# New orders of the steps on every engine of a four-layer network kernel on one core

## The reference

```python
x = _layernorm(x + _L0_attn_ref(x, ...))   # 16 heads of 64, softmax attention
x = _layernorm(x + _L0_ffn_ref(x, ...))    # hard routing: best of 8 clusters, best of its 8 tiles, spline of that tile
x = _layernorm(x + _L1_attn_ref(x, ...))   # linear attention and attention in a window of 65, gated; out @ wo + bo + x
x = _layernorm(x + _L1_ffn_ref(x, ...))    # causal attention with normalised q and k, then a mixture of 8 experts
```

## Time and profile before

| what | us |
|---|---|
| median of 3 runs | 2324.85 (2324.02 to 2327.23) |
| the profiled execution, its own time | 2327.11 |
| span of its trace | 2325.3 |
| mean granted clock of TensorE | 0.989 of full speed |
| PE busy | 2189.3 (94%) |
| DVE busy | 1605.0 (69%) |
| ACT busy | 1352.6 (58%) |
| POOL busy | 849.2 (37%) |

### The profile page before, as it was taken

One profiled execution on the slowest core, in us unless ns is written; L12 is line 12 of the kernel. 1 busy time (PEld: TensorE's weight loads), 2 busy tenths in 40 slices (PEclk: granted clock), 3 DMA queues, 4 the chain that ended last, 5 costly groups with the idle time before them and its releaser, 6 DMA issues.

```text
span 2325.3 us, 44711 instructions
## 1 busy us (share of the span) xinstructions
PE 2189.3 (94%) x16091; PEld 1523.0 (65%) x16091; DVE 1605.0 (69%) x5015; ACT 1352.6 (58%) x3784; POOL 849.2 (37%) x1010
## 2 busy tenths in 40 slices
PE   8989999999999999999999999999999999999897
PEld 5656666856668566676667665676666756667465
DVE  5666686686766866678765878658686686766752
ACT  5336574765647755476555767466564764646452
POOL 3314561054510654107521256114561054510630
PEclk9999999999999999999999999999999999999999
DMA  4000001010010100110001100001001010010001
GB/s 153 28 1 1 1 2 46 11 33 1 1 55 2 33 1 1 55 33 1 1 10 46 33 1 1 28 28 33 1 1 46 10 33 1 2 42 6 33 1 50
DMA packets 24726, 50.48 MB, mean 22 GB/s; under 512 B 3316, under 2 KB 3900, under 8 KB 24252
## 3 DMA queue, kind: packets, MB, share of 16 engines
q1 hardware_dynamic: 24508, 47.63, 6.3%
HBM read 45.52 MB, written 2.10 MB: 20 GB/s over the span
## 4 chain that ended last, share of the span: by engine, by line
PE 81%; DVE 9%; ACT 5%; POOL 3%; issue 1%; DMA 0%; SPq 0%; DVEq 0%; ACTq 0%
PE ps L1488 10%; PE ps L1509 10%; PE ps L601 5%; PE ps L667 5%; PE ps L650 4%; PE ps L1521 4%; PE ps L867 4%; PE ps L1422 4%; PE ps L1439 4%; PE ps L905 4%; PE ps L1394 3%; PE ps L798 3%; PE ps L781 3%; PE ps L834 3%; PE ps L1383 2%; PE ps L605 2%
## 5 line engine op out<-in xcount | busy, mean ns | idle before, releaser
L1047 POOL TENSOR_TENSOR rstd<-ve,half_neg 128x4 f32<-128x4 f32 (+1 forms) x56 | 66.8, 1193 | 972.4 <-DVE ve L1028 972.4
L1509 PEld LDWEIGHTS ps<-wbuf,QK 128*128 128x128 f32 x2048 | 265.4, 191 | 108.2 <-issue 103.3
L1304 POOL TENSOR_TENSOR E<-E,ri 128x512 f32<-128x512 f32 x240 | 249.4, 1041 | 149.7 <-DVE ri L1102 148.8
L1612 ACT ACTIVATE QK<-ps,cols 128x512 f32<-128x512 f32 x256 | 173.9, 687 | 219.3 <-PE ps L1488 218.9
L1738 POOL TENSOR_TENSOR work<-work,ri 128x128 f32<-128x128 f32 x480 | 231.6, 506 | 108.7 <-DVE ri L1661 107.0
L1488 PE MATMUL ps<-h2T,wbuf 128*128 128x512 f32 x512 | 270.9, 617 | 0.1
L1509 PE MATMUL ps<-wbuf,QK 128*128 128x128 f32 x2048 | 269.0, 275 | 0.0
L928 ACT ACTIVATE E<-ps,nm 128x256 f32<-128x256 f32 x480 | 224.5, 479 | 57.9 <-DVE nm L1095 56.9
L1731 POOL TENSOR_TENSOR rn<-ss,half_neg 128x8 f32<-128x8 f32 x120 | 196.0, 1638 | 156.5 <-DVE ss L1637 154.0
L1572 ACT ACTIVATE work<-ps,nm 128x128 f32<-128x128 f32 x480 | 200.2, 433 | 66.9 <-DVE nm L1653 66.0
L1653 DVE CUSTOM_DVE_ANT_0 ps<-ps,causal 128x128 f32<-128x128 f32 (+1 forms) x512 | 167.5, 389 | 31.0 <-PE ps L1422 30.1
(11 more groups left out here) (280 smaller groups left out, 4558.6 us busy)
## 6 DMA issues: line engine op xcount, KB each, us to landing
wbuf<-in_w SPq DMA_DIRECT2D x128, 256.0 KB, 3.2
xT<-in_xT SPq DMA_DIRECT2D x8, 256.0 KB, 3.5
xr<-in_xr SPq DMA_DIRECT2D x8, 256.0 KB, 3.8
bias_t<-in_bias_t SPq DMA_DIRECT2D x1, 2048.0 KB
out_y<-xn SPq DMA_DIRECT2D x8, 256.0 KB, 2.1
wqkv<-in_wqkv SPq DMA_DIRECT2D x1, 1536.0 KB
wo<-in_wo SPq DMA_DIRECT2D x2, 512.0 KB, 7.8
rows<-in_rows SPq DMA_DIRECT2D x1, 531.0 KB, 6.6
```

The source lines that it names most:

```text
L1304: nc.gpsimd.tensor_tensor(L.E[:, g % 4, :, :], L.E[:, g % 4, :, :], L.ri[:, g, :].unsqueeze(2).broadcast_to((P, NT, S)), ALU.mult)\
L1509: last = nc.tensor.matmul(bank2[2 + x % 2][:, t * P:(t + 1) * P], hid[:, x % 2, c, t * P:(t + 1) * P], w2[:, x % WB, c, :], start=(c == 0) ...
```

## The change

Only digits in `ORDER` differ: the tables of the joined parts for all five engines, and those of the last part for vector, tensor, scalar and gpsimd. The tables of part 0 are as they were. Every table keeps its length and its count of each digit, so every engine issues the same instructions in each part, and each half keeps its own order; only the interleaving is another. Entries that differ, of all: joined parts vector 132 of 458, tensor 104 of 337, scalar 90 of 294, gpsimd 36 of 95, sync 2 of 12; last part vector 58 of 229, tensor 64 of 176, scalar 52 of 157, gpsimd 14 of 53. Counted along a table, no step is moved by more than two steps of the other half.

```diff
--- before.py
+++ after.py
@@ -59,45 +59,45 @@
...
     ("both", "vector"):
-        "010001111011010101011110001111110110111111110110100111101110011111010100110110100010101101010011"
-        "110101110100001101101000011110011000100101010110110111111111011101111111111111011111111011110111"
-        "111011111011110011010000111100001001110100001101101000101100101010011100101000101101001001011010"
-        "001101000100101010100100000011111101111110001000000000000001000000000000100000110000000000000000"
-        "010100000110000100000110001010000100000000101011111110101100001001000010",
+        "001000101111101101101110001111110110111111101101100111101111011101001101001111000010111001100011"
+        "110011101100010110101000110101001010100011100110111011110111111101111111111111011111111101111110"
+        "111101110111101011010000101110001010110100010011101001011100010010010111010000101101001001010110"
+        "001010100110010101000110000001111101101010110100000000000000000000100000100000001000001000000000"
+        "100000010000100010010101101000000000010001011101011110101100000101000010",
     ("last", "vector"):
-        "000000010000001011101001011101010100110111101010101111111111101100001111101001011010100010010101"
-        "101001000111010001011011000101101100100110110010011011001001110100010111001001010100101010000000"
+        "000000000001001011101010111011010001101101011010111111110110111010111010110100101001010100001011"
+        "011000100111010001011011001001101100010111010010011011001001110100010111010001101000100110000000"
...
     ("both", "tensor"):
-        "010011111011011100101101011101110101110110101110010101010100111101010110101101010110010101110001"
-        "101011111011101011111011011101101110110110101110100101100010111101001010110101010011001010110101"
-        "001101001010110101010101010100111001100101111111111111101111111110111100110110110011000000000000"
-        "0000010000000100000000202000020000202200222222",
+        "001101101111011100101101101101101011110110110110010100110101101101011101001101010011011001011110"
+        "010101110111011011111101110101101110110110110101100010111101011100010100101011101010110010010101"
+        "001011010010110011011001011000101101100101111111111110111111111101111101001111010011000000000000"
+        "0000000010001000000000202000002000202202022222",
     ("last", "tensor"):
-        "000010010010010110110101000111010110110111111100110011011000100101001110100101010101100101101010"
-        "010110100101100101101010101000011100110000000000000000000000000000000000000000",
+        "000100001010001111011010101100101010111111110110001011000110110100101100001110100110100101100101"
+        "011010101010110001010011011000010111010000000000000000000000000000000000000000",
...
     ("both", "scalar"):
-        "110110001111010101011110111001111100100011111100011110000111101110100101110000101101101111111011"
-        "101011111111101111011110101100111010111010010110100110110001101010010110100011101001101001010110"
-        "011010100111011111111011111111111110111010111010101010000000000000000000000000000000022202022222"
+        "110010111110100101111100101011101110101101011010011010010101111110100011100101110100111101111110"
+        "101111011111110111110101101101101010111000101110001111001001011001010110010101100011011010011011"
+        "100100010110111111101111111111111101111010110110101010000000000000000000000000000000020220222222"
         "222",
     ("last", "scalar"):
-        "000000001001110101010011011011100111011101011001111000001011100101101010011100000111100101101100"
-        "00111001011010110010000000000000001000000000000000000000000",
+        "000000100011010101101100101101011011101011010011011010010110101001011010010110100101100101011001"
+        "00111010011011001001001000000000000000000000000000000000000",
...
     ("both", "gpsimd"):
-        "000110110111100001010111010110101010111111111111100110101001101010101001100101011010000010010",
+        "000111011011100001101001110101110001111111111111101010011011010001110001010101011001000001100",
     ("last", "gpsimd"):
-        "000101101101110011010100101010101100101101010100000",
+        "000101101101110011010010110100110101001011001100000",
     ("both", "sync"):
-        "1111101111",
+        "1101111111",
 }
 KINDS = ["first", "both", "both", "last"]
```

## The result

The changed kernel takes 2336.4 us in the median of its runs (2332.14 to 2346.52), the kernel before, beside it, 2327.37 us (2320.91 to 2336.36). The ratio is 1.0044, 95% interval 1.0027 to 1.0062: it is slower, by 6 to 14 us. The forecast was +7.2 us, to 2332, with a range of 2319 to 2342.

A forecast was written before the change was run, and what follows sets the result against it. The prediction took TensorE as the bound, busy 2189.3 of 2325.3 us. It summed 5.1 - 0.7 + 2.8 = +7.2 us onto the 2324.85 us median, giving 2332 us, with an 8-in-10 range of 2319 to 2342.

The forecast's parts named there:

- signs of being wrong: L899 starting with L650's end, L899 to L1422 over 0.5 us shorter, change mostly in last part, or other fall counts.
- (b): Opening of joined parts: power ahead of L1304 moves the POOL/DVE conflict; 0.1 us gained a part, 0.7 us in all.
- (a): End of joined parts 1 to 6: L601 between the L856 steps delays L899; 6 x 0.85 = 5.1 us lost.
- (c): Dense stretches of joined parts: new waits such as L867 on L1304; 0.4 us a part, 2.8 us lost.
- (d): Routing in the middle of joined parts: L718 two expert steps earlier, inputs just ready; cost 0, at most 0.5 a part.
- (e): Last part: opening bound by POOL's sixteen L1731, whose order stays; 0, with 1 us to either side.
- the clock falls at the boundary: Rival: wider PE wait at six boundaries halves the clock behind L899; up to 1.7 us each, +10, 2342 us; chance 0.15.

The follow-up runs named there:

- e1: Kernel before with only the new tail of the joined parts' tensor table (an L601 step between the two L856); ratio 1.0046, +7.2 us at equal clock.
- e2: Changed kernel with the old tail put back in the joined parts' tensor table; ratio 1.0018 to the kernel before, +0.4 us at equal clock.
- e3: Kernel before with two steps of the program ahead (four L601 pairs) between the two L856 steps; ratio 1.0087, +12.0 us at equal clock.
- e12: Changed kernel with idle PE matmuls in five idle places of each joined part; ratio 1.0006 to the kernel before, +7.1 us at equal clock.
- e7: Kernel before, old tables, with idle PE matmuls in five idle places of each joined part; ratio 0.9971, -1.2 us at equal clock.
- e5: Kernel before with the new tail alone, plus three idle matmuls ahead of the wait before L899; ratio 1.0060, +5.7 us at equal clock.
- e6: Kernel before with the double tail, plus six idle matmuls ahead of the wait before L899; ratio 1.0106, +11.2 us at equal clock.
- e9: Kernel before, old tables, with three idle matmuls (0.73 us) among the experts of each joined part; ratio 1.0053, +5.9 us at equal clock.
- e8: Kernel before, unchanged, profiled a second time; 2329.67 us.
- e10: Kernel before, old tables, with seven idle matmuls (1.7 us) among the experts of each joined part; ratio 1.0065, +11.0 us at equal clock.

## Why the prediction was right, and where it was not

The direction, the size and the place were right: +7.2 us forecast, +5.9 at equal clock, 1.0044 in all. That the +10 us of the ratio also lie near +7.2 is in part luck: the forecast had no clock in its sum. Two of its own signs of being wrong came: the first L1422 stands 0.54 us earlier in a part (under (b)), and the profile has more falls, ten in the joined parts against six. Neither touches the term that carries the sum.

(a) *The end of a joined part* is the cause, shown by one table entry alone (e1), by its removal (e2) and by twice the dose (e3). The forecast said 6 x 0.85 = 5.1 us; the wait grew by 5.0, and by 10.2 for the double. Part 7, without the program ahead, did not grow (281.0 us after 281.3), as said; one execution tells that to about 0.7 us only, since e1's part 7, with the old order inside and the same two falls, took 282.0. What made it readable in advance was the 0.06 us between DVE's last L1038 and L899 in the earlier trace rows. Nothing of the earlier L601 came back, as said.

(b) *The opening* was right in its mechanism, but its gain was put too small. L1394's wait for L1643 fell by 3.1 us, seven times 0.43, as worked out from the earlier trace rows. L867's wait for POOL's L1304 rose by 2.4 us, seven times 0.35. The forecast said only that it would not shrink. These two come to the 0.1 us a part of the forecast, but they are not the whole opening. The forecast put the end of the earlier trace rows at 786.0 after 786.07, as POOL is full; POOL's two L1304 came earlier too:

```profile
793.89 2.04 POOL L1304 TENSOR_TENSOR E<-E,ri 128x512 f32<-128x512 f32 x2
...
794.99 0.66 PE L867 MATMUL ps<-ident,E 128*128 128x128 f32 x4 [0.54 <-POOL E L1304]
```

This L867 stands 24.6 us into its part (from 770.4), where that of the earlier trace rows stood at 25.0 (from 761.1): 0.4 us gained, not 0.1. The first L1422 of a part came at 26.74 us after 27.28. DVE's L1637 of 0.81 us is gone, and a later one is held up behind an L1304 instead (timeline of after):

```profile
787.68 1.04 POOL L1304 TENSOR_TENSOR E<-E,ri 128x512 f32<-128x512 f32 x1
...
788.31 0.44 DVE L1637 TENSOR_SCALAR ss<-ss 128x8 f32<-128x8 f32 x1
```

That agrees with the rule of the Trainium skill, page SBUF — State Buffer, section "Who interferes with whom", as the prediction used it: the L1637 begun at 788.31 ends with POOL's L1304 (787.68 + 1.04 = 788.72), at 788.75. The conflict is moved, not removed.

(c) *New waits in the dense stretches*, 0.4 us a part and 2.8 in all, came as waits and not as time. One of its two named places came exactly, the second L1252 behind four L1712:

```profile
1024.77 1.12 DVE L1712 SCALAR_TENSOR_TENSOR acc<-ps,gl,acc 128x128 f32<-128x128 f32 x4
...
1025.80 0.68 DVE L1252 TENSOR_TENSOR E<-ps,bias_t 128x512 f32<-128x512 f32 x1
...
1026.63 1.16 PE L798 MATMUL ps<-kloc,GQ 32*128 32x128 f32 x16 [0.16 <-DVE E L1252]
```

The 0.16 us are the 0.17 worked out. The other, L867 of 812.67, came ready: no wait stands there. In joined part 5, at full clock in both kernels, there are three more small ones (0.12 and 0.14 us of L1521 for ACT's L1580, 0.1 us more of L867 for ACT's L937), so the new waits come to some 0.5 us a part. Yet the sum inside a part is nothing, by the parts without a fall: 278.70 us with the tail alone and 278.70 with all new tables. The place of the same instruction in part 5 of both kernels shows how: with the new tables PE is 0.4 us earlier at 25 to 45 us into the part, level at 105, 0.3 earlier at 153 (L700) and 0.05 earlier at 254. What failed is thus the sum of (b) and (c): +0.3 us a part was forecast, -0.05 came. A list of moved steps shows the places where a wait may be new; those where the same shift takes one away have to be listed with the same care.

The section on the change says that no step is moved by more than two steps of the other half. Counted again along the strings, some go further: up to 7 in the tables of the vector engine, 5 or 6 in those of the tensor engine, 12 for one entry of the last part's scalar table. Its table lengths are also two or three too high (the vector table has 456 entries, the tensor table 334). The counts of entries that differ are right.

(d) *The routing* was right: L718 did not wait.

(e) *The last part* was put at 0 with 1 us to either side. It costs 1.1 us (the changed kernel against e3) to 1.5 us (e12 against e7). The prediction looked at the opening only and took the rest as unmoved. In both pairs the two kernels are within 0.4 us of each other 47 us into the part, and the cost has come by 72 us: it lies in the causal attention (L1439, L1521), behind the opening.

With the sizes measured: 6 x 0.8 for joined parts 1 to 6, -0.3 for part 7 and +1.3 for the last, +5.8 us; the equal-clock column has +5.9. That they meet so closely is luck, as part 7 and the column show above.

The rival *the clock falls at the boundary* was right as a mechanism. In the profile of the changed kernel it shows at one of the six boundaries, with e1 and e12 at 8 of 18. Of the rest between +5.9 and the +10 us of the ratio, 2.7 us are clock by the table and 1.1 us the choice of the runs of before (2328.6 us in the mean of those beside the changed kernel, 2329.7 in the table). How much of it the boundary falls make is not settled. Filling the boundary took those falls away (e5, e6) and gave no time back that the runs can show, and a part that is 0.7 us longer without any new wait lost as much clock (e9). What the runs show is that falls come behind the same idle places (about 98 and 151 to 160 us into a part) in some parts and not in others, that filling the places makes them fewer (e7), that a second execution of the same kernel meets others (e8), and that a changed length of the parts goes with other numbers and lengths of falls (3.4 us up to 13.7). A rule for that was not found.

## What to carry to other kernels

When a program is only reordered, look for the chain whose last link has no room before the bound engine's next work (here 0.06 us) and ask of each table whether anything was put into that chain; one entry there outweighs hundreds elsewhere. Set beside a list of possible new waits a list of those that the same shift takes away; here both were about 0.5 us a part. And when all orders are equal within a few us, filling the bound engine's idle places with work that nobody reads can be worth more than any order: here -8.4 us, where the new orders cost 10.

## What was not expected of the hardware

- The time of a run goes with its granted clock, 1.77 us for each 0.001 over 194 runs. A fall of 3.4 us to 0.50 costs 1.7 us where PE is full (280.40 against 278.70 us in e1), and less elsewhere (1.4 us in part 4 of the changed kernel, 280.1 against 278.7).
- Behind an idle place of about 0.9 us that two others surround, the clock fell in some executions and parts and not in others (e8: 280.80 and 277.80 us for the same instructions). It also fell where PE had been busy 3.18 of 3.40 us (e7).
- Falls of 13.7 us came in e6, e9 and e10 at the place where 3.4 us were the rule. PE was busy 12.83 of 13.60 us in one of them, and the part took 284.50 us instead of 278.50.
- Thirteen idle bf16 matmuls in each joined part raised the mean clock from 0.9869 to 0.9907 and the kernel got 6.7 us faster; with a few more, 0.9923.
